# Two mixtures of experts in a hybrid kernel, run over all tokens at once or in two groups of two sequences

## What is computed

```python
probs = softmax(einsum('btd,de->bte', x, gate_w))          # 8 experts
w, idx = top_k(probs, 2); w = w / w.sum(-1, keepdims=True)
for i in range(8):
    wi = where(idx == i, w, 0.0).sum(-1)
    h = silu(x @ w1[i]) * (x @ w3[i])                       # 128 -> 512
    out = out + (h @ w2[i]) * wi[..., None]                 # 512 -> 128
x = x + retention(layernorm(x))
x = x + mixture(layernorm(x))
x = x + attention(layernorm(x))
x = x + mixture(layernorm(x))
```

## Time and profile before

| | us |
|---|---|
| median of 3 runs | 978.31 (971.21 to 979.86) |
| profiled execution | 975.61 |
| its span | 973.7 |
| mean granted TensorE clock | 0.859 of full speed |

### The profile page before, as it was taken

One profiled execution on the slowest core, in us unless ns is written; L12 is line 12 of the kernel. 1 busy time (PEld: TensorE's weight loads), 2 busy tenths in 40 slices (PEclk: granted clock), 3 DMA queues, 4 the chain that ended last, 5 costly groups with the idle time before them and its releaser, 6 DMA issues. The chain is left out here.

```text
span 973.7 us, 19729 instructions
## 1 busy us (share of the span) xinstructions
PE 708.3 (73%) x6652; PEld 481.4 (49%) x6652; DVE 582.6 (60%) x1765; ACT 344.0 (35%) x597; POOL 327.1 (34%) x654
## 2 busy tenths in 40 slices
PE   1688889688997421999922699787877984299990
PEld 0355556345565321999811244443433442298990
DVE  7977834787814580677650666656548732366664
ACT  2223143334243410444314055354344461143340
POOL 0122210123342275577736000202212222366771
PEclk9999999799997555999956589989779995599996
DMA  9201199111020011555426500600600000154554
GB/s 209 78 23 44 46 213 172 55 46 65 24 59 1 11 52 50 155 164 162 142 92 153 133 4 3 144 3 20 146 6 15 13 16 8 50 159 135 158 155 137
DMA packets 99848, 80.89 MB, mean 83 GB/s; under 512 B 7663, under 2 KB 91698, under 8 KB 99010
## 3 DMA queue, kind: packets, MB, share of 16 engines
q1 hardware_dynamic: 95206, 70.25, 29.1%
q0 software_dynamic: 4544, 9.38, 2.9%
HBM read 54.44 MB, written 23.40 MB: 80 GB/s over the span
## 5 line engine op out<-in xcount | busy, mean ns | idle before, releaser
L1208 DVE TENSOR_REDUCE rmax<-PA 128x1 f32<-128x512 f32 (+3 forms) x256 | 120.7, 489 | 96.9 <-PE PA L1893 89.7
L751 POOL DMA_INDIRECT outs_dram<-va,ids x78 | 91.5, 1173 | 57.2 <-POOL ids L747 30.2
L736 POOL DMA_INDIRECT rows_dram<-va,idx x64 | 63.8, 997 | 123.4 <-DVE va L1091 105.6
L1850 PE MATMUL PC<-ffn_w,pm 128*128 128x128 f32 x624 | 88.3, 285 | 7.3 <-DMA ffn_w<-in_w 6.6
L1893 PE MATMUL PA<-kst,qst 96*128 96x512 bf16 (+3 forms) x256 | 85.0, 337 | 0.0
L1891 PE MATMUL PA<-mqb,idb 128*128 128x128 bf16 x256 | 60.7, 238 | 30.2 <-DMA qst<-qst 15.0
L1850 PEld LDWEIGHTS PC<-ffn_w,pm 128*128 128x128 f32 x624 | 76.5, 193 | 10.4 <-DMA ffn_w<-in_w 9.6
L1138 DVE SCALAR_TENSOR_TENSOR pm<-PB,invb,decay 128x512 f32<-128x512 f32 x78 | 58.0, 744 | 38.8 <-ACT decay L1474 38.1
L1618 PE MATMUL P<-const,xn 128*128 128x128 f32 x92 | 19.3, 346 | 80.1 <-ACT xn L1409 32.3
L704 POOL COPY va<-vs 128x128 f32<-128x128 f32 x32 | 12.9, 402 | 188.9 <-DVE vs L880 188.9
L1466 ACT ACTIVATE kv_b<-P 128x256 f16<-128x256 f16 x78 | 29.9, 383 | 129.7 <-PE P L1829 129.7
(11 more groups left out here) (244 smaller groups left out, 1558.9 us busy)
## 6 DMA issues: line engine op xcount, KB each, us to landing
ffn_w<-in_w SPq DMA_DIRECT2D x78, 256.0 KB
rows_dram<-wall SPq DMA_DIRECT2D x1, 8385.0 KB, 47.0
X<-in_w SPq DMA_DIRECT2D x32, 256.0 KB, 2.9
proj_w<-rows_dram SPq DMA_DIRECT2D x78, 65.0 KB
qst<-parts_dram SPq DMA_DIRECT2D x12, 384.0 KB
kst<-parts_dram SPq DMA_DIRECT2D x12, 384.0 KB
parts_dram<-qkp SPq DMA_DIRECT2D x16, 256.0 KB, 2.7
X<-in_x SPq DMA_DIRECT2D x8, 256.0 KB, 5.4
```

What stands on the lines that cost most here:

```text
L736: nc.gpsimd.indirect_dma_start(out=rows_dram, out_offset=bass.IndirectOffsetOnAxis(ap=idx[:, t, r:r + 1], axis=0), in_=xrow[:, t, :], in_o ...
L751: nc.gpsimd.indirect_dma_start(out=outs_dram, out_offset=bass.IndirectOffsetOnAxis(ap=ids[:, k % YB:k % YB + 1], axis=0), in_=ysb[:, k % Y ...
L1208: nc.vector.tensor_reduce(rmax[:, i, h % HG:h % HG + 1], PA[:, n % 2, 0:(i + 1) * P], AX_X, ALU.max).then_inc(pair_sb[n % 2], 1)
L1850: ins = mm(PC[:, k % 2, 0:D], eT[:, k % 2, f, :], w2b[k % WB2][:, f, :], start=f == 0, stop=f == FB - 1)
```

## The change

The tokens of a mixture are taken in two groups of two sequences, each with its own rows, counts, tables and 23 tiles (16 + 7), so 46 tiles in a mixture and 92 in the kernel. Groups are numbered 0 to 3 through both mixtures. On every engine a function `beside(g, n)` is called behind tile n of group g and holds what is done next to the tiles:

- Group 0: counts of sequence 2, the leaving norm, norm and routing of sequence 3, choices of sequences 2 and 3 (now `choose_weights` and `choose_rows`), their row scatters (tiles 4 to 7 and 17 to 20), and group 1's tables (`table_counts`, `table_rows`).
- Group 1: reading back and combination of sequences 0 and 1 (now `first_picks` and `second_picks`), their LNC norms, projections, parts and values, and sequence 0's parts and stacks on SyncE (tiles 17 and 18).
- Attention: combination, norm and front of sequences 2 and 3 within sequence 0's part; routing, choices and row scatters of sequences 0 and 1 for the second mixture, and group 2's tables.
- Group 2: the last weighting and the output projection of sequence 3, routing of sequences 2 and 3, scatters (tiles 8 to 11 and 17 to 20), group 3's tables.
- Group 3: reading back and combination of sequences 0 and 1, and their results.

Before the first tile stand the choices of sequences 0 and 1 and 16 row scatters; routing of sequence 0 now lies before the last feed-forward add. The leaving norms are taken by the list `LEAVE`.

In the loop itself: the two id operations move from POOL to VectorE (`out_rows`), the copy of the result moves from VectorE to ScalarE (`expert_out`), the turned tile uses P6 alone and the down matmuls one half of PC alone. P7 and the other half of PC (`side_bank`) serve the work beside the tiles. `silu_a` moves to another place in SBUF.

```diff
+SPG = 2
+GROUPS = SEQ // SPG
+HALF = ROWS // GROUPS
+NTL = PICKS * SPG * TPS + E - 1
...
+LEAVE = (((0, 0),), ((0, 1), (1, 0)), ((1, 1),), ((0, 2),), ((0, 3), (1, 2)), ((1, 3),))
...
+        side_bank = (P7[:, :], PC[:, 1, :])
...
+            def parts(s):
...
+            def outs_in(m, s):
+                c = m * SEQ + s
+                if s % SPG == 0:
+                    for b in range(YB):
+                        sp.wait_ge(y_out[b], 16 * len(range(b, (c // SPG + 1) * NTL, YB)))
+                if m == 0 and s >= 1:
...
+            def beside(g, n):
+                if g == 1:
+                    if n == 4:
+                        outs_in(0, 0)
+                    if n == 9:
+                        outs_in(0, 1)
+                    if n == 17:
+                        parts(0)
+                    if n == 18:
+                        stacks_in(0)
+                if g == 3:
+                    if n == 4:
+                        outs_in(1, 0)
+                    if n == 6:
+                        outs_in(1, 1)
...
+            def tiles(g):
+                sp.wait_ge(tables, g + 1)
+                sp.wait_ge(rows_out[g], 16 * PICKS * SPG * TPS)
+                for n in range(AHEAD):
+                    rows_in(g, n)
+                for n in range(NTL):
+                    w2_load(g, n)
+                    if n + AHEAD < NTL:
+                        rows_in(g, n + AHEAD)
+                    beside(g, n)
...
-            experts(0)
-            stacks(0)
-            stacks(1)
+            tiles(0)
+            tiles(1)
+            parts(1)
+            outs_in(0, 2)
             for g in range(NG * SEQ):
                 maxima(g)
...
             def scatter_outs(k):
-                n = k % NTL
-                pool.wait_ge(x_in[k % XB], 16 * (k // XB + 1))
-                if k >= YB:
-                    pool.wait_ge(y_out[k % YB], 16 * (k // YB))
-                s1, token = xb[:, k % XB, D:D + 1], xb[:, k % XB, D + 1:XROW]
-                link(nc.gpsimd.tensor_scalar(idf[:, :], s1, ownp[:, n:n + 1], token, ALU.is_equal, ALU.add))
-                nc.gpsimd.tensor_scalar(ids[:, k % YB:k % YB + 1], idf[:, :], const[:, C_PAD + k % YB:C_PAD + k % YB + 1],
-                                        None, ALU.max).then_inc(ids_sb, 1)
                 pool.wait_ge(ids_sb, k + 1)
                 pool.wait_ge(y_sb, k + 1)
                 nc.gpsimd.indirect_dma_start(
...
+            def part_first(s):
+
+                wait_front(pool, "k", A + s)
+                nc.gpsimd.tensor_tensor(qkt_att, qkf[:, :, :], qkp[:, 0, :, :], ALU.subtract).then_inc(qt_sb, 1)
...
+            def beside(g, n):
+                if g == 0:
+                    if 4 <= n < 4 + TPS:
+                        scatter_rows(0, 2 * TPS + n - 4)
+                    if 17 <= n < 17 + TPS:
+                        scatter_rows(0, 3 * TPS + n - 17)
...
+                if g == 1:
+                    for s, first in ((0, 6), (1, 11)):
+                        if n == first:
...
+                    if n == 14:
+                        part_first(0)
+                    if n == 15:
+                        part_last(0)
...
+            for t in range(SPG * TPS):
+                scatter_rows(0, t)
+            leave_blocks(SEQ - 1)
+            for k in range(GROUPS * NTL):
+                scatter_outs(k)
+                beside(*divmod(k, NTL))
...
+                def out_rows(k):
+                    g, n = divmod(k, NTL)
+                    dve.wait_ge(x_in[k % XB], 16 * (k // XB + 1))
                     if k >= YB:
                         dve.wait_ge(y_out[k % YB], 16 * (k // YB))
-                    dve.wait_ge(m2_ps, k + 1)
-                    nc.vector.tensor_copy(ysb[:, k % YB, :], PC[:, k % 2, 0:D]).then_inc(y_sb, 1)
...
+                def beside(g, n):
+                    if g == 0:
+                        if n == 2:
+                            choose_weights(0, 2)
+                        if n == 3:
...
+                        if n == 15:
+                            choose_weights(0, 3)
+                        if n == 16:
+                            choose_rows(0, 3)
+                        if n == 17:
+                            table_counts(1)
+                        if n == 18:
+                            table_rows(1)
...
+                    route_compare(0, 1)
...
+                    if k > first:
+                        out_rows(k - 1)
+                    beside(*divmod(k, NTL))
+                out_rows(end - 1)
...
+                def expert_out(k):
+                    if k >= YB:
+                        act.wait_ge(y_out[k % YB], 16 * (k // YB))
+                    act.wait_ge(m2_ps, k + 1)
+                    nc.scalar.activation(ysb[:, k % YB, :], PC[:, 0, 0:D],
...
+                    if g == 1:
+                        for s, first in ((0, 10), (1, 16)):
+                            if n == first:
+                                normalize(LNC, s)
+                            if n == first + 1:
+                                side_turn(LNC, s)
+                            if n == first + 2:
+                                side_part(s, 0)
+                            if n == first + 3:
+                                side_part(s, 1)
+                            if n == first + 4:
+                                side_values(s)
+                            if n == first + 5:
...
+                    if k > first:
+                        expert_out(k - 1)
+                    beside(*divmod(k, NTL))
...
-                    bank = ring_bank[k % 2][:, 0:D].bitcast(F16)
+                    bank = P6[:, 0:D].bitcast(F16)
                     pe.wait_ge(x_in[k % XB], 16 * (k // XB + 1))
-                    if k >= 2:
-                        pe.wait_ge(xt_sb, k - 1)
+                    if k >= 1:
...
-                    if k >= 2:
-                        pe.wait_ge(y_sb, k - 1)
+                    if k >= 1:
+                        pe.wait_ge(y_sb, k)
                     for f in range(FB):
-                        ins = mm(PC[:, k % 2, 0:D], eT[:, k % 2, f, :], w2b[k % WB2][:, f, :], start=f == 0,
-                                 stop=f == FB - 1)
+                        ins = mm(PC[:, 0, 0:D], eT[:, k % 2, f, :], w2b[k % WB2][:, f, :],
+                                 start=f == 0, stop=f == FB - 1)
...
+                    if g == 1:
+                        for s, first in ((0, 11), (1, 17)):
+                            if n == first:
+                                side_turn(LNC, s)
+                            if n == first + 1:
+                                channels(A + s, "q", side("q", A + s)).then_inc(side_ps, 1)
+                            if n == first + 2:
+                                channels(A + s, "k", side("k", A + s)).then_inc(side_ps, 1)
+                            if n == first + 3:
+                                token_values(s, side("v", s)).then_inc(side_ps, 1)
```

More of the change, by code:

```diff
@@ L1493, in experts @@
[L1493 to L1503 removed]
+                    high_rows(0, 1)
@@ new lines, in experts @@
+                    keep_counts(0, 0, ring("count", 0, 0)).then_inc(ring_sb, 1)
+                    exp_logits(0, 1)
+                    keep_counts(0, 1, ring("count", 0, 1)).then_inc(ring_sb, 1)
+                    leave_normalize(4)
+                    plain_turn(LNM1, 2)
+                    keep_logits(0, 2, ring("router", 0, 2)).then_inc(ring_sb, 1)
+                    high_rows(0, 2)
+                    exp_logits(0, 2)
+                first, end = m * GROUPS * NTL, (m + 1) * GROUPS * NTL
@@ L1504, in experts @@
+                tile_turned(first)
+                for k in range(first, end):
+                    if k + 1 < end:
                         tile_turned(k + 1)
                     gate(k)
-                if m == 0:
-                    for s in range(2):
-                        normalize(LNC, s)
-                        front(A + s)
-                        second_part(s)
-                    normalize(LNC, SEQ - 2)
-                    normalize(LNC, SEQ - 1)
+                    if k > first:
+                        expert_out(k - 1)
+                    beside(*divmod(k, NTL))
@@ L1514, in attention @@
+                expert_out(end - 1)
             def attention():
@@ L1863, in experts @@
-                wait_ring(pe, "count", m, SEQ - 1)
-                first, end = m * NTL, (m + 1) * NTL
+                    pe.wait_ge(ring_sb, len(RING))
+                    pe.wait_ge(in_att, in_att_n)
+                else:
+                    pe.wait_ge(ao_raw, 2 * SEQ - 1)
+                first, end = m * GROUPS * NTL, (m + 1) * GROUPS * NTL
                 turn_tile(first)
```

855 lines of the change are left out of this document (534 added, 321 removed).

## The result

The changed kernel takes 991.77 us (median of 4 runs, 987.58 to 994.87) against 977.17 for the kernel before: ratio 1.0155, 95% interval 1.0092 to 1.0218. It is slower, by 1.6%, with an interval that lies on both sides of 2%. Its profiled execution has a span of 993.0 us, 19.3 more than the one of before; it is the slowest of its four, and the medians are 14.6 us apart.

The account below looks back on a forecast made before the run. TensorE nearly full in the two tile loops, VectorE's in-order chain equally 2.40 us a tile, and 171 us of other stretches to hide. Gains of 139.5 against costs of 166.5 us, net +27, gave 1003 us, range 960 to 1037.

Parts of the forecast that it names:

- (a): Start of the first loop: fewer row scatters ahead and earlier routing of sequence 0, 36 us less.
- (b): Stretch between first loop and attention (486 to 538 us) vanishes, 52 us less.
- (e): Attention: two combinations and norms added, one sequence's norm and routing leave, 1 us more.
- (1): Both tile loops: 92 tiles against 78, cycle 2.55 us instead of 2.40, cost 36 us (27 by the lower bound).
- faster rival: Transfers and scatters keep up and the clock stays up: net -12 or -21 us, 957 to 966; chance 0.25.
- (2): Both mixtures' loops: VectorE's moved work is added whole, cost 47.5 us; nothing if VectorE had slack.
- (3): Group switch: POOL's row scatters of sequence 3 among output scatters, 9 us twice, cost 18 us (each 4 to 12).
- (4): Split projections: ScalarE's second part waits behind POOL's subtraction and holds PE, 4 us each, cost 8 us (0 to 12).
- (5): Sequence 0's stacks issued at tile 18 ahead of down weights, cost 17 us (2 to 20).
- (6): Side work of PE and ACT beside the loops, table switches included, cost 17 us (5 to 22).
- (8): Clock: matmuls at 1.2 instead of 2.4 GHz behind stalls and VectorE's holes, cost 17 us (0 to 60).
- The gate as a rival: Clock at 1.2 GHz in more than half of the tiles: 30 to 60 us more, 1033 to 1065; chance 0.09.

Follow-up runs that it names:

- the extra instruction: One more VectorE reduction per tile (128x128 to one column, result unused): kernel before 976.27 us, ratio 0.9994; changed kernel 995.71 us, ratio 1.0193.
- the few-picks run: Changed kernel with the combination of sequences 2 and 3 in the first mixture cut to one of four token tiles: 1010.71 us on the third chip, ratio 1.0114.
- first experiment: Changed kernel with the two id operations back on POOL, everything else kept: 998.71 us, ratio 1.0197.
- without the late scatters: Changed kernel without the row scatters of sequence 3 in both mixtures: 965.95 us, ratio 0.9843.
- the spread run: Changed kernel with sequence 0's six stack transfers issued one at a time behind tiles 18 to 22 and the loop: 976.72 us, ratio 0.9974.
- the last kernel: Changed kernel with spread stacks, shifted front and second parts, late transposes, sequence 3's scatters four at a time, ids around the product: 990.49 us, ratio 0.9900.

## Why the prediction was right, and where it was not

The direction, the mechanism and most terms held: predicted 1003 us with 960 to 1037, measured 991.77, +19.3 us between the profiled executions against +27. The closeness of the total is luck in part: costs that were put too high by 21.5 us stand against an attention that was put too low by 11, and the range was 77 us wide. One of the prediction's own signs of being wrong came true (attention longer by more than 5 us).

**What it gives.** (a) 36.0 for 36, (b) 50.8 for 52, (c) 43.4 for 44, (d) 7.5 for 8.5. These were differences between landmarks, and each was met within 1.2 us; for (a) that is luck in part, since the variants with the same start would give 36 to 43. (e) failed: the attention is 12.0 us longer, not 1. The term took two combinations and norms of 3.5 us as mostly hidden because VectorE was busy for 43.4 of 68 us there. The first eighth of the weighted matmuls went from 23.2 to 30.1, which is 7 of the 12 and the size of that work. It is 27.3 to 30.1 in the changed kernels with all of it in place and 23.0 in the kernel before with the extra instruction, so 4 to 7 us are there in every pair; that they are VectorE's added work was argued, and the few-picks run (26.3) does not show it. Some 4 to 5 go when the parts come a tile later (attention 269.9), by a way that no run isolates. The cause of the longer attention stays open.

**What it costs.** (1) 92 plain periods: 2.52 against my 2.55, so 45 x 2.52 x 2 = 226.8 between products, 33.3 more than before, for 36. Without the id operations the period is 2.33 to 2.40 (first experiment), so they cost 0.13 to 0.19 us a tile. That the link costs was right: it holds the register load back by 0.18 us. Taken apart around the product the link is gone, but the first operation costs as much ahead of the product. The lower bound is worked out wrong: a cycle of 2.40 gives 3.6 + 45 x 2.40 + 2.0 = 113.6 us a loop and 22.5 us, not 27, and with it the low edge of the faster rival is 4.5 us lower.

(2) VectorE's moved work, 47.5 "added whole". In groups 0 to 3 most tiles with work beside take 3.4 to 5.5 us and not 2.52. The half of 33.5 and half of 13.8 make 23.7 and not 23.9, which changes nothing. The rule behind it ("no place") is refuted for a small instruction: 0.28 us a tile are free in plain tiles of both kernels, under the register load. In tiles with work beside it holds: there the same instruction adds 0.19 us, and TensorE's idle time before the up matmuls (37.2 us for 0.3) ends with VectorE's copy. No run takes the moved work away, so its full price is not measured by itself. Of the 145 us, 33.3 are tiles, 23.8 the switches and 19.9 the two periods at the stacks (18.19 and 6.75 against 2.52); 68 are left for all moved work with its waits and its clock, where terms 2, 4, 6, 7 and 8 together had 95.5.

(3) Group switch, 9 each within 4 to 12. Measured: periods of 14.5 and 14.3, 12.0 and 11.8 over a plain one; without the late scatters 10.6 and 11.2 us less. Of the costs it was the one most undersized, by 6 us over both.

(4) Parts, 4 each: one wait of 4.86 us on ScalarE and 4.31 on TensorE was there; the run with later parts took 5.6 us out of the loop for the 8.

(5) Stacks, 17: the wait of 13.28 for weights and one of 4.50 behind it; spreading them took 11.4 us out of the trace and 1.8% off the ratio. Mechanism shown, size within the bounds.

(6) Side work of TensorE and ScalarE, 17: too large. The table switches cost nothing where I had put 3. The tiles that carry this work are mostly ones in which VectorE is late anyway, so by the periods the same microseconds were counted twice; no run removes the rest of this work.

(8) Clock, 17: too large as well. The granted clock in the four groups is 0.89, 0.90, 0.93 and 0.97; the up matmuls' mean rose from 224 ns to 226 and 227, the down matmuls' from 285 to 293. 2 x 1104 x 2.5 ns + 736 x 8 ns = 11 us of busy time, part of it inside waits. It does drop where I said (1.49 us behind the switch), and the next tile is back at 0.83. (The prediction compared 1.85 us for eight down matmuls, a figure of the timeline, with 0.96, one of the chain; the timeline's own is 1.11 to 1.16, so its 1.55 is 0.15 to 0.2 too large.) The gate as a rival (0.09) didn't come.

Together (1) to (8) were 166.5 and are 145.0; (2), (4), (6), (7) and (8) carry the surplus between them (95.5 for 68), most of it by my reading in (6) and (8), and the attention took 11 of it back.

**The rivals.** The faster one named its conditions rightly: with the stacks not holding the weights (the spread run) the kernel is level with before, 0.9974, and with the switch's scatters gone it is 0.9843. Neither holds in the kernel as it is. The forecast of what would show it: first up matmul "near 351" (351.0 here, 343.8 to 350.9 in other kernels with the same start), period 2.52 to 2.59 (2.52), loops of 165 to 180 us each (183.5 and 155.0: mean right, split wrong), a weights wait of over 5 us (13.28) at tile 20, ScalarE waiting on POOL's subtraction (4.86), clock below 0.9 in the loops (one of four), attention longer by more than 5 us as a sign of being wrong (12.0, so here it was). TensorE's holes on VectorE's account are there, but are 1 to 2.9 us long and not 3.

## What to carry to other kernels

Work moved beside a tight loop is paid on the in-order engine that closes the loop; count what is moved in microseconds of that engine and compare with the gap it leaves, before counting the gap as won. Here 171 us of mostly idle stretches shrank by 138 and the loops grew by 145. In a pipeline cut into groups, look for the resource that must finish all of a group before the next may begin (here POOL's scatters, 11 us a switch), and for any large transfer on the queue that feeds the loop: break it into pieces. And stalls that are cheap to remove one by one can cover each other: here the parts and stacks together gave no more than the stacks alone.

## What the runs showed of the hardware that was not expected

An instruction placed directly ahead of a register load on VectorE (0.276 us, 76 and 90 times) was free in tiles with nothing else beside: the load's "issue" fell from 0.57 to 0.40 us and from 0.61 to 0.42. In tiles with work beside it added 0.19 us. What delays the load is a wait ahead of it: the scale came 0.85 to 0.87 us behind the end of the product, or of the first id operation where the program has VectorE wait for that (medians of the changed kernel and three variants). Rows that stand back to back in a timeline are no proof of a full engine.

In the last kernel TensorE's matmuls came two or three at a time, with over a microsecond between, while nothing in the profile held them (timeline of PE, during POOL's burst of row scatters):

```profile
427.46 0.27 PE L2188 MATMUL PA<-kv_b,pm 128*128 128x128 f16 x2 [1.16 <-issue]
428.88 0.37 PE L2188 MATMUL PA<-kv_b,pm 128*128 128x128 f16 x2 [1.15 <-issue]
430.33 0.48 PE L2188 MATMUL PA<-kv_b,pm 128*128 128x128 f16 x3 [1.08 <-issue]
```

TensorE's waits marked "issue" ahead of the first up matmuls add up to 15.9 us in the changed kernel (14 times, the longest 2.9) and to 25.5 in this one, against 0.3 us for that line before. A label "issue" does not mean that the engine waited for no other: the 15.9 us each end 0.10 us behind VectorE's copy of the weights, as do 18 us or more of the 25.5, and without the late scatters they are as many (16.1). Some 6 us, in the two bursts of scatters of the last kernel (427 to 431 and 899 to 902), end with nothing that the trace shows, as in the rows above. What slows TensorE there stays open; no run isolates it.
